# Two streams of segments of a six-layer decoder, merged in another order

## The reference

```
x = _layernorm(x + _L0_attn_ref(x, ...))            # layer a: rotary attention, 16 heads, Taylor weights 1 + s + s*s/2
x = _layernorm(x + _L0_xattn_ref(x, ctx, ctx, ...)) # layer b: cross attention with a mask, softmax
x = _layernorm(x + _L0_ffn_ref(x, ...))             # layer c: 8 experts of 512 hidden, top-2 gate, all experts computed
x = _layernorm(x + _L1_attn_ref(x, ...))            # layer d: delta rule, short and long causal filters, a gate over 4 paths
x = _layernorm(x + _L1_xattn_ref(x, ctx, ctx))      # layer e: cross attention without projections, softmax
x = _layernorm(x + _L1_ffn_ref(x, ...))             # layer f: gated MLP of 704 hidden with 4-bit block quantisation
return x
```

## Time and profile before

| | |
|---|---|
| Time, median of 3 runs | 4396.55 us (4383.08 to 4405.46) |
| The profiled execution's own time | 4401.85 us |
| Its span, first to last instruction | 4399.9 us |
| PE busy | 3407.8 us, 77% |
| VectorE busy | 2618.4 us, 60% |
| ScalarE busy | 1639.0 us, 37% |
| GpSimd busy | 315.0 us, 7% |
| DMA, mean over the span | 40 GB/s |
| Mean granted clock of TensorE | 0.887 |
| Chain that ended last | PE 49%, VectorE 25%, issue 11%, ScalarE 7%, GpSimd 5% |

### The profile page before, as it was taken

How to read it: one execution, slowest core, us unless ns; L and a number is a source line. 1 busy time by engine, 2 the same in 40 slices (tenths; PEclk the granted TensorE clock), 3 DMA queues, 4 the chain that set the end, 5 groups by cost and what they waited for, 6 DMA issues and landing times.

```text
span 4399.9 us, 64768 instructions
## 1 busy us (share of the span) xinstructions
PE 3407.8 (77%) x22532; PEld 2643.9 (60%) x22532; DVE 2618.4 (60%) x5927; ACT 1639.0 (37%) x3066; POOL 315.0 (7%) x696
## 2 busy tenths in 40 slices
PE   1687878787887878788787888878788887878854
PEld 0465757566675756567575666657566665756652
DVE  4336484756748475674847557484665738466553
ACT  1333333443333434333334433333433333444311
POOL 1001010100101010010101001010100101010010
PEclk7788989899999989999898899999889899989966
DMA  2020111101111110101111011111001111100100
GB/s 84 1 68 25 63 33 63 32 23 45 30 63 33 63 32 25 44 28 63 32 63 32 16 48 33 63 32 63 18 22 57 33 63 32 51 22 29 52 13 3
DMA packets 183454, 175.67 MB, mean 40 GB/s; under 512 B 58952, under 2 KB 147680, under 8 KB 183136
## 3 DMA queue, kind: packets, MB, share of 16 engines
q1 hardware_dynamic: 183136, 171.27, 12.2%
HBM read 156.55 MB, written 14.68 MB: 39 GB/s over the span
## 4 chain that ended last, share of the span: by engine, by line
PE 49%; DVE 25%; issue 11%; ACT 7%; POOL 5%; DMA 2%; SPq 1%; DVEq 0%; PEldq 0%; PEld 0%; ACTq 0%; POOLq 0%
PE bank L699 27%; DVE region L1790 8%; PE bank L733 6%; PE bank L787 3%; DVE region L1749 2%; ACT pt_f L1194 2%; PE bank L754 2%; PE bank L767 2%; POOL region L679 2%; POOL region L677 2%; DVE nm_f L1571 2%; ACT split_f L1205 1%; PE bank L708 1%; PE bank L1013 1%; DMA gram_scratch<-region 1%
## 5 line engine op out<-in xcount | busy, mean ns | idle before, releaser
L1194 ACT ACTIVATE pt_f<-bank 128x512 f32<-128x512 f32 x768 | 416.0, 595 | 274.8 <-PE bank L767 274.1
L699 PE MATMUL bank<-xTb,c_w 128*128 128x256 f32 x2048 | 498.3, 401 | 0.0
L699 PE MATMUL bank<-c_w,region 128*128 128x256 f32 x2048 | 465.6, 381 | 0.0
L1790 DVE SCALAR_TENSOR_TENSOR region<-vpad,cols,region 128x256 f32<-128x256 f32 x1024 | 451.9, 483 | 16.0
L699 PEld LDWEIGHTS bank<-xTb,c_w 128*128 128x128 f32 x2048 | 408.7, 203 | 69.7 <-issue 10.4
L1723 DVE SCALAR_TENSOR_TENSOR yb<-bank,comb,yb 128x256 f32<-128x256 f32 x256 | 112.1, 479 | 531.3 <-PE bank L699 531.3
L1293 ACT ACTIVATE region<-bank,cols 128x256 f32<-128x256 f32 x512 | 212.8, 470 | 568.2 <-PE bank L699 568.2
L699 PEld LDWEIGHTS bank<-c_w,region 128*128 128x128 f32 x2048 | 384.8, 190 | 51.7 <-issue 0.2
L733 PE MATMUL bank<-identb,split_f 128*102 128x128 bf16 (+1 forms) x4096 | 315.8, 248 | 101.6 <-DVE split_f L1556 81.0
L733 PEld LDWEIGHTS bank<-identb,split_f 128*102 128x102 bf16 (+1 forms) x4096 | 300.2, 149 | 131.6 <-issue 85.4
L767 PE MATMUL bank<-qT_f,kT_f 102*128 102x256 bf16 (+1 forms) x1536 | 281.7, 284 | 121.3 <-ACT pt_f L1194 97.0
(11 more groups left out here) (305 smaller groups left out, 5744.8 us busy)
## 6 DMA issues: line engine op xcount, KB each, us to landing
c_w<-in_c_w SPq DMA_DIRECT2D x256, 512.0 KB, 4.6
gram_scratch<-region SPq DMA_DIRECT2D x16, 512.0 KB, 2.6
x<-in_x SPq DMA_DIRECT2D x16, 256.0 KB, 4.4
ctxf<-in_ctx SPq DMA_DIRECT2D x16, 256.0 KB, 4.6
ctxb<-in_ctx SPq DMA_DIRECT2D x16, 256.0 KB, 6.8
out_dram<-x SPq DMA_DIRECT2D x16, 256.0 KB, 2.2
region<-gram_scratch SPq DMA_DIRECT2D x128, 8.0 KB
inverse_scratch<-region SPq DMA_DIRECT2D x32, 64.0 KB
```

The source lines that it names most:

```text
L699: mm = pe.matmul(out_ap, l, r, start=(i == 0), stop=(i == len(pairs) - 1))
L1194: act.activation(dst, PS[use].rearrange("p (c s) -> p c s", c=c), func, **kw).then_inc(*PS.drained(use))
L1790: ins = dve.scalar_tensor_tensor(dst[:, c, :], x, w_[:, c, k:k + 1], dst[:, c, :], ALU.mult, ALU.add)
```

## The change

Only `BODY`, the merged list, is another one. The order within each stream stays, and so do all instructions, buffers and semaphores. Relative to the segments of the other stream, half of the segments move by one or two places (some by more).

```diff
@@ -97,15 +97,15 @@
 BODY = """
-c_in c_gate c_comb e_in e_part1 c_up0 e_part2 c_up1 c_down0 e_turnq c_up2 e_turnk c_down1 c_up3 c_down2 e_max0 c_up4
-c_down3 e_max1 c_up5 e_max2 c_down4 c_up6 c_down5 e_max3 c_up7 e_shift e_again c_down6 e_score0 c_down7 c_res e_score1
-e_weigh0 e_score2 e_weigh1 e_score3 e_weigh2 e_weigh3 c_apply d_in e_out a_norm d_proj e_res a_proj e_apply f_in
-a_rope d_conv f_up0 a_part1 d_silu f_up1 a_part2 d_token a_turnq f_round0 d_norm a_turnk d_chan d_gram d_blocks f_round1
-d_grams f_down d_fir0 f_res f_apply d_place a_score0 d_fir1 a_score1 a_weigh0 a_score2 a_weigh1
-d_fir2 a_score3 a_weigh2 a_weigh3 d_fir3 a_out b_in d_one4 d_fir4 b_ctx a_res d_two4 a_apply
-d_one5 d_fir5 b_x b_proj d_two5 b_part1 d_one6 b_part2 d_fir6 b_turnq d_two6 b_turnk d_sums d_scan0 d_scan1 b_max0
-d_scan2 b_max1 d_scan3 b_max2 d_turn d_gate b_max3 d_gated b_shift b_again d_logit d_weight d_mix b_score0 b_score1
-b_weigh0 b_score2 b_weigh1 d_ms b_score3 b_weigh2 b_weigh3 d_out b_out d_res b_res b_apply d_apply
+c_in c_gate c_comb e_in c_up0 e_part1 c_up1 c_down0 c_up2 c_down1 e_part2 c_up3 c_down2 e_turnq e_turnk c_up4 c_down3
+e_max0 c_up5 e_max1 c_down4 e_max2 c_up6 e_max3 c_down5 c_up7 e_shift e_again c_down6 e_score0 c_down7 c_res e_score1
+e_weigh0 e_score2 c_apply e_weigh1 e_score3 e_weigh2 e_weigh3 e_out d_in a_norm e_res d_proj a_proj e_apply f_in
+a_rope d_conv f_up0 a_part1 d_silu f_up1 a_part2 d_token a_turnq f_round0 d_norm a_turnk d_chan f_round1 d_gram f_down
+f_res d_blocks f_apply a_score0 d_grams d_fir0 d_place a_score1 a_weigh0 a_score2 a_weigh1 a_score3 d_fir1 a_weigh2
+d_fir2 d_fir3 a_weigh3 a_out b_in d_one4 d_fir4 b_ctx a_res d_two4 a_apply d_one5 b_x d_fir5 b_proj d_two5 b_part1
+d_one6 b_part2 d_fir6 d_two6 b_turnq d_sums d_scan0 b_turnk d_scan1 b_max0 d_scan2 b_max1 d_scan3 b_max2 d_turn d_gate
+b_max3 b_shift d_gated b_again d_logit d_weight d_mix b_score0 b_score1 b_weigh0 d_ms b_score2 b_weigh1 b_score3
+b_weigh2 b_weigh3 d_out b_out b_res b_apply d_res d_apply
 """.split()
```

## The result

The changed kernel takes 4471.13 us in the median of 4 runs (4465.36 to 4473.69), the kernel before 4399.63 us (4383.08 to 4405.46) beside it: a ratio of 1.0167 with a 95% interval of 1.0137 to 1.0197. Forecast were 4417 us and a range from 4360 to 4450. The direction was right, the size was not: +72 us instead of +20.5.

A forecast was written before the change was run, and what follows sets the result against it. PE bound the expert part, VectorE the stretch from a_out to b_turnq; terms summed to +1.25 us over 14 iterations (+17.5) plus about 3 in the seventeenth, some +20.5: 4417 us in the median, range 4360 to 4450.

The forecast's parts named there:

- front: c_up0 to e_weigh3: PE's matmuls stay without a gap and the wait at e_again goes, -0.35 us an iteration.
- middle (2.8 + 0.8): a_turnk to d_fir3 and DRAM round: VectorE reaches a_out 2.8 us later; d_one4's new wait costs 0.8 through the clock.
- scan: At b_turnq: d_two6 moves into PE's 3.04 us wait for VectorE, -2.3 us an iteration, bounds 0 and -4.
- end: b_res ahead of d_res: b_y up to 0.5 us earlier, VectorE's jump back less hidden; +0.3 us, bounds -0.5 and +2.2.
- its own signs of being wrong: Wrong if d_one4 starts at once, d_fir3 is not later, or c_up0 drops to 7.2 us.
- the jump back on VectorE shows: Rival at the loop's end: +1.9 us more an iteration, +27 us, 4444 us; chance 0.12.
- The step on VectorE: f_round1 to d_fir3: f_round1 starts at 2384.6, d_grams and d_fir0 move later, d_fir3 ends at 2417.8 instead of 2414.98.
- The step on DRAM: d_gram starts 6.7 us later; round of 28.26 us is ready at 2416.7, so d_one4 waits about 3.2 us.
- the 2.3 us of slack: At a_y: PE ends at 2425.2, VectorE wants it at 2427.5, so at full clock d_one4's wait is hidden.
- The clock's part of the prediction: Behind d_one4's new wait PE runs at the lower clock, losing 2.2 to 3.9 us, making 0 to +1.5; +0.8 taken.
- The bound of -4: Scan term's far bound at b_turnq, us an iteration: the four iterations with the long d_two6 keep the full clock.
- filling waits keeps PE's clock up: Rival at c_up0 and b_turnq: c_up0 -2.2 us, long d_two6 -1.2 in the mean; -38 us, 4358; chance 0.21.

The follow-up runs named there:

- the end alone: Kernel before with only b_res and b_apply put ahead of d_res at the end of the list: 4444.38 us, ratio 1.0106.
- either half alone: Kernel before with only VectorE's d_grams and d_fir0 moved later (4477.01 us), or only d_gram's DRAM round behind f_round1, d_fir1 to d_fir3 ahead of f_apply (4494.16 us).
- VectorE's work displaced: Kernel before with d_grams and d_fir0 moved behind f_apply and a_score0, d_gram and d_blocks left ahead of f_round1: 4477.01 us, ratio 1.0174.
- the scan alone: Kernel before with only d_two6 put ahead of b_turnq and d_scan0 ahead of b_turnk: 4343.88 us, ratio 0.9867.
- the hint: Prefetch hint on every engine's backward loop branch: 4379.09 us on the kernel before with the new end, 4467.46 us on the changed kernel.

## Why the prediction was wrong, step by step

The forecast beside two measures: a part's difference of medians divided by 14, and the mean length of its fourteen iterations in its trace less the 257.56 us before. The first also holds what happens outside the loop, the second is one execution.

| term | forecast, us an iteration | medians | trace |
|---|---|---|---|
| front | -0.35 | -0.9 | -0.4 |
| middle (2.8 + 0.8) | +3.6 | +7.4 | +7.1 |
| scan | -2.3 | -4.2 | -3.5 |
| end | +0.3 | +3.0 | +2.5 |
| sum of the parts | +1.25 | +5.4 | +5.8 |
| the changed kernel | +1.25 | +5.1 | +5.2 |

Two steps failed. The prediction took the jump back on VectorE for all but hidden, and it hid PE's new wait for the round through DRAM in a slack that did not exist. None of its own signs of being wrong came up: they asked whether d_one4 waits and d_fir3 is later, and both did, only more so.

**The end failed as a choice between its bounds.** The prediction gave -0.5 for a free jump and +2.2 for one that shows, and took +0.3 "as d_res lands within the old wait". The old wait was 2.81 us, for PE's c_gate. But the jump takes 2.8 us too, and before, both ended at about the same moment: VectorE was through at 2237.35, 2.81 us before 2240.16. There was no room in that wait. When VectorE's last operation ends 3.28 us after c_in (2277.35 - 2274.07) instead of 0.51, c_comb is late by the whole difference, 2.75 us. An idle stretch names what ended it last and hides what else ran out in it. The gain of 0.5 us in b_y's half came in the changed kernel (from b_out to c_in 8.0 us instead of 8.5), but with the end alone it is a loss of 0.8 (9.3 us), as b_y runs at the slow clock there in ten of fourteen iterations. The rival "the jump back on VectorE shows" had the right mechanism at a chance of 0.12; its price, the +2.2 bound, is three quarters of what the end alone costs; the slow b_y was in neither.

**The middle had the two chains in the wrong roles.** The step on VectorE, measured from f_round1's start: forecast 2417.8 - 2384.6 = 33.2 us to the end of d_fir3, measured 2456.74 - 2424.81 = 31.9. It was better than forecast, since a_score0 is shorter than the 3.9 us given it: d_grams' matmuls begin 1.8 us behind f_down's end, so a part of a_score1 had been counted with it. The step on DRAM, from f_round1's start to the blocks' arrival: forecast 2416.7 - 2384.6 = 32.1 us, measured 2459.75 - 2424.81 = 34.9. Three pieces lengthen it: the store of the products left 4.7 us behind f_round1's start instead of 3.8, as d_gram's matmuls took 2.08 us at 1.2 GHz and not 1.16; GpSimd's root of f_res stood ahead of the inversion, as the prediction said it might, which puts its start from 6.9 us behind the store to 8.3; and the inversion took 13.7 us instead of 11.3, because it now runs beside the filters. One gave 1.9 us back, as the prediction said it might. SyncE's queue in the last iteration with layer d before, from which the 28.26 us were read:

```profile
4198.95 0.41 SPq L571 DMA_DIRECT2D out_dram<-x  x1
4199.41 1.21 SPq L555 DMA_DIRECT2D inverse_scratch<-region  x2
```

The inversion had ended at 4197.49, and its store left 1.9 us later, behind the store of the output. In the changed kernel that store is out before, and the inverses leave 0.03 us after the inversion's end. The way back itself is the same: 8.0 us from their first store to d_one4 there, 8.2 here. The queues were looked at in the prediction, the slower inversion was not: its time was taken as a constant from an iteration in which the thirty taps began only behind it, at 4198.84, and it took 11.6 us.

So PE's wait at d_one4 is 6.47 us and not 3.2, and the 2.3 us of slack that were to hide it do not exist: VectorE is 1.3 us earlier, the wait 3.3 us longer, and d_one4 behind it takes 3.51 us at a clock of 0.54. VectorE waits 3.65 us for PE. That the first step came out 1.3 us better than forecast did not help, since it was not the later one. The clock's part of the prediction held (a slow group behind a long wait, as by the rule that it took from the Trainium skill, TensorE: Matmul & The Clock Gate, section HAM oscillation), its conclusion did not, as it was set against slack that was gone. The rule does not hold for every wait here: behind the same 2.85 us f_up1 ran at a clock of 1.00 and of 0.62. The table of two by two says the same of the whole middle: either half alone costs 83 us and both 104.

**The slow clock reached further than the groups costed.** f_down after a second halt in the kernel with VectorE's work displaced (+2.25 us), f_up1 in the changed kernel (6.69 us, 5.00 before) and d_one5 there (3.61 us, 2.35 in the changed kernel) are none of the places that the prediction priced.

**The scan was right in mechanism and place, too small in size.** d_two6 now stands ahead of b_turnq, whose wait is 0.85 us in the kernel with this part alone. It gained 3.4 us in a typical iteration. 2.2 of them are the ones forecast: from b_turnq's start to b_max0 7.54 us instead of 9.73, as d_two6's 2.00 are out of it. The other 1.2 come ahead of b_turnq, where the order is the old one and PE's groups are faster: c_up0's 32 matmuls take 8.92 us instead of 9.79, and with them and d_proj PE is 0.85 us earlier at f_round1. Why the clock is granted so is not shown; part of the gain was luck. (The prediction read d_two6 as 2.15 us in nine of thirteen iterations and 3.67 in four. In the loop it is 2.00 in nine of fourteen, 2.15 and 2.33 in one each and 3.67 in three; the mean of the term would be -2.2.) The bound of -4 was nearest, by the medians. In the changed kernel the order gains less in that place, since b_turnq there waits for nothing and d_two6 takes 3.48 us (2.00 in the kernel with the scan alone).

**The front** was right, and its -13 us are not all its own: in the loop of its trace it gains 0.41 us a time against 0.35 forecast. The rest lies outside of the loop, most of it ahead of it (4.3 us), where the scan alone is 3.7 and the end alone 6.1 us shorter, too.

The rival "filling waits keeps PE's clock up" was right in kind for the scan part, at c_up0 as well, but too large: it gave c_up0 -2.2 us, the scan alone brought -0.9. In the changed kernel c_up0 got no shorter, 10.02 us for 32 matmuls (9.45 in the earlier trace rows).

What stays open: which waits put the loop into the pattern with the slow f_up1 (the hint's gain in the changed kernel goes there), what sets the settled lengths of 252.6 and 262.8 us, what the jump costs in the kernel before (the hint was never tried with the old end), and what the late round costs by itself with f_apply in its old place.

## What to carry to other kernels

Before you fill an idle stretch, ask what else was running out in it: the releaser named is the last one only, and a jump back of a loop leaves a trace only once nothing covers it. Compare two delays that meet at one instruction before you add them; a chain through DRAM has its own length, and that length depends on what runs beside its slowest engine. A segment that needs nothing (a filter over data long there) belongs ahead of one that waits for another engine's queue: that one move, with d_two6 into PE's wait, gave 2.0%, more than any larger reordering tried here.

## What the hardware showed that was not expected

- VectorE's jump back to the top of the loop costs 2.8 us from its last operation to the next, and 0.6 us with the hint on the backward jump. Where PE waits for VectorE right behind it, this is worth 57 us over thirteen jumps (+42 against -15); where the clock takes it back, 4 to 15 us.
- GpSimd's small operations of L679, on 64 partitions, take 288 ns in the mean and 391 ns beside VectorE's filter taps; the filters themselves take 14.21 us for thirty instead of 13.71.
- The same wait can be followed by either clock: behind 2.85 us f_up1 takes 5.00 us at 1.00 or 7.99 us at 0.62 in one kernel, and behind 0.99 or 1.00 us b_y takes 3.28 us at 0.58 with the end alone and 2.00 us in the changed kernel. A price read from one iteration's slow group holds for that iteration.
- Three kernels settle at an iteration of 262.8 us (the changed one, it with the hint, and VectorE's work displaced alone) and four at 252.6, each from a different order; a change of 2 us inside an iteration may leave its length as it was.
